# Two-layer attention with experts and a spiking FFN: two heads' outputs packed in 32 rows, another order of the attention slot, one Sigmoid pass for spikes, the last normalisation on GpSimd

## What is computed

```python
x = x + L0_xattn(layernorm(x), ctx, ctx)      # softmax attention, 16 heads of width 8, with biases
x = x + L0_ffn(layernorm(x))                  # 8 experts, top 1, silu, 128 -> 512 -> 128
x = x + L1_xattn(layernorm(x), ctx, ctx, positions, mask)
x = x + L1_ffn(layernorm(x))                  # spiking
```

```python
m = max(scores);  e = exp(scores - m);  attn = e / (1.0 + sum(e))
out = (attn @ V) @ W_o.T
```

```python
mem_new = 0.9 * mem + y - (mem > 1)           # from mem = 0
spk = (mem_new > 1)
result = sum of the five spk / 5
```

## Time and profile before

| | us |
|---|---|
| median of 3 runs | 438.39 (435.57 to 439.0) |
| the profiled execution | 439.88 |
| its span | 438.0 |
| PE busy | 344.5 (79%) |
| DVE busy | 309.1 (71%) |
| ACT busy | 268.8 (61%) |
| POOL busy | 136.8 (31%) |
| mean granted clock of PE | 0.878 |

### The profile page before, as it was taken

One profiled execution on the slowest core, in us unless ns is written; L12 is line 12 of the kernel. 1 busy time (PEld: TensorE's weight loads), 2 busy tenths in 40 slices (PEclk: granted clock), 3 DMA queues, 4 the chain that ended last, 5 costly groups with the idle time before them and its releaser, 6 DMA issues.

```text
span 438.0 us, 9507 instructions
## 1 busy us (share of the span) xinstructions
PE 344.5 (79%) x3230; PEld 205.2 (47%) x3230; DVE 309.1 (71%) x840; ACT 268.8 (61%) x473; POOL 136.8 (31%) x238
## 2 busy tenths in 40 slices
PE   1589999999897625999932679999999888796762
PEld 0233454445343514999920224545444343575751
DVE  5787999998957365466514777999998752268764
ACT  2128988889767201665511148898988785367776
POOL 4423123534002005644037455444642101011000
PEclk9999999999979855899975556999999995889996
DMA  5134342333201402554112122111221000000001
GB/s 150 55 84 127 101 121 67 108 106 88 65 4 53 138 19 43 144 146 100 42 51 67 56 60 59 49 47 49 60 68 56 5 6 1 0 1 13 15 22 48
DMA packets 35920, 27.36 MB, mean 62 GB/s; under 512 B 5936, under 2 KB 31920, under 8 KB 35872
## 3 DMA queue, kind: packets, MB, share of 16 engines
q1 hardware_dynamic: 32896, 23.51, 18.7%
q0 software_dynamic: 1248, 2.56, 2.7%
q10 hardware_dynamic: 1728, 0.66, 0.6%
HBM read 14.19 MB, written 4.13 MB: 42 GB/s over the span
## 4 chain that ended last, share of the span: by engine, by line
PE 55%; DVE 18%; ACT 11%; issue 6%; DMA 5%; POOL 4%; SPq 0%; ACTq 0%; DVEq 0%; POOLq 0%
PE M L338 14%; PE S L287 11%; DVE nm L656 9%; PE S L1234 5%; PE S L1253 4%; ACT Pt L513 3%; PE S L1410 3%; PE M L446 2%; PE M L454 2%; PE M L346 2%; DMA sorted_y<-ysb 2%; PE M L1426 2%; ACT spike L1472 2%; PE M L409 2%; PE S L1434 1%
## 5 line engine op out<-in xcount | busy, mean ns | idle before, releaser
L656 DVE TENSOR_REDUCE nm<-S 128x2 f32<-128x512 f32 x256 | 164.5, 686 | 31.3 <-PE S L287 29.1
L513 ACT ACTIVATE Pt<-S 128x1024 f32<-128x1024 f32 x128 | 130.3, 1019 | 35.8 <-PE S L296 33.7
L287 PE MATMUL S<-Kt,Qt 32*128 32x256 f16 x512 | 86.9, 303 | 18.3 <-DVE nm L656 8.4
L296 PE MATMUL S<-Qt,Kt 32*128 32x256 f16 x512 | 79.1, 290 | 0.0
L338 PE MATMUL M<-Pt,Vt 128*32 128x256 f32 x1024 | 74.5, 412 | 1.5 <-ACT Osb L500 0.9
L287 PEld LDWEIGHTS S<-Kt,Qt 32*128 32x128 f16 x512 | 25.1, 95 | 74.4 <-DVE nm L656 49.1
L338 PEld LDWEIGHTS M<-Pt,Vt 128*32 128x32 f32 x1024 | 28.0, 114 | 29.4 <-issue 6.5
L632 POOL TENSOR_TENSOR rstd<-ve,mhalf 128x2 f32<-128x2 f32 x24 | 17.8, 743 | 63.0 <-DVE ve L610 62.4
L1279 ACT ACTIVATE hf<-S,b1c 128x128 f32<-128x128 f32 x92 | 26.1, 369 | 18.4 <-PE S L1234 18.4
L815 POOL TENSOR_TENSOR q_lo<-qf,q_hi 128x256 f16<-128x256 f32 x15 | 10.1, 671 | 74.5 <-ACT q_hi L546 74.5
L1151 POOL DMA_INDIRECT xt<-normed_x,source x23 | 22.4, 974 | 34.6 <-DVE source L1069 17.0
(11 more groups left out here) (173 smaller groups left out, 574.0 us busy)
## 6 DMA issues: line engine op xcount, KB each, us to landing
w_ff<-in_w SPq DMA_DIRECT2D x8, 512.0 KB, 3.9
ctxT<-in_ctxT SPq DMA_DIRECT2D x16, 128.0 KB, 2.6
Pt<-in_mask SPq DMA_DIRECT2D x8, 256.0 KB, 3.0
Qt<-q_hi SPq DMA_DIRECT2D x28, 64.0 KB, 1.9
Kt<-k_hi SPq DMA_DIRECT2D x28, 64.0 KB, 1.9
sorted_y<-ysb SPq DMA_DIRECT2D x23, 64.0 KB, 2.7
Kt<-k_lo SPq DMA_DIRECT2D x16, 64.0 KB, 1.9
Qt<-q_const SPq DMA_DIRECT2D x16, 64.0 KB, 2.6
```

What stands on the lines that cost most here:

```text
L287: mm = pe.matmul(S1[h % 2][:, q, :], Qt[b % NBUF][rows_of(h), h // HG, q * P:(q + 1) * P], Kt[b % NBUF][rows_of(h), h // HG, :], start=Tru ...
L296: mm = pe.matmul(S2[pair % 2][:, hh, k, :], Kt[b % NBUF][rows_of(h), h // HG, k * P:(k + 1) * P], Qt[b % NBUF][rows_of(h), h // HG, :], st ...
L513: act.activation(Pt[i // 2][:, 2 * j:2 * j + 2, :].rearrange("p a n -> p (a n)"), S2[i % 2][:, :, :, :].rearrange("p a k n -> p (a k n)"), ...
L656: v.tensor_reduce(nm[par][:, h // 8, :, h % HG, h // HG % 2], S1[h % 2][:, :, :], AX.X, ALU.max, negate=True)\
```

## The change

Five things change.

1. **Packing.** Two groups of heads share a block of 32 rows, 16 for each. Vt has a new layout, so that `pv` of the second group adds into the same rows as the first. The four `pv` of a tile all go to M[1]. ACT copies the bank once, 128x512, where it copied four times 128x256. Four transposes follow where there were eight, and one reciprocal and one multiplication of double width. The rows of wo and the bias of V are put into the order of `packed_order()` on the host.
2. **PE's order.** The transposes of the outputs all stand after pair 1. `op` and `v` follow pair 4, `op` first. The next `m_turn` follows pair 5, then `pv` 0; `pv` 1 follows pair 6, `pv` 2 pair 7 and `pv` 3 the first pair of the next slot.
3. **ACT's and DVE's order.** kf and k_hi stand ahead of aT. ACT takes the copy of V, behind exp(4), and the copy of the maxima behind it. DVE adds to X behind r(4); the moments stand behind r(5).
4. **Spikes.** One Sigmoid of `SPIKE * mem - (SPIKE + 128)`, written in f16 with SPIKE = 1.75 * 2**30, takes the place of Relu and Sign; it stands first in ACT's slot, and is cut in two for the last tile. One more table is loaded on ACT.
5. **The last normalisation.** xn of the FFN is made on POOL. PE's wait for the last X moves from before the first h to before y.

```diff
             def pv(b, par, g):
                 pe.wait_ge(ly["exp_done"], 8 * b + 2 * g + 2)
-                if g == 0:
-                    pe.wait_ge(ly["v_copied"], b + 1)
+                tile, sub = g // 2, g % 2
                 for k in range(QT):
                     for i in range(HG):
-                        mm = pe.matmul(M[O_BANK[g]][32 * i:32 * i + 32, 0:S], Vt[par][:, k, HG * g + i, :],
-                                       Pt[g][:, i, k * S:(k + 1) * S], start=(k == 0), stop=(k == QT - 1))
+                        at = (k * NPK + tile) * 2 * (HG * KB + KH) + sub * HG * KB + i * KB
+                        mm = pe.matmul(M[1][KB * i:KB * i + KB, tile * S:(tile + 1) * S], Vflat[par][:, at:at + KB],
+                                       Pt[g][:, i, k * S:(k + 1) * S], start=(sub == 0 and k == 0),
+                                       stop=(sub == 1 and k == QT - 1))
...
                 pair(4)
-                if nxt and ly["bias"]:
-                    next_m_turn()
-                if cur:
-                    if old:
-                        pe.wait_ge(ly["aT_copied"], b)
-                    elif ly["bias"]:
-                        pe.wait_ge(ly["ob_made"], 1)
-                    pv(b, par, 0)
-                if nxt and ly["position"]:
-                    next_m_turn()
-                pair(5)
...
                 if old:
-                    if cur:
-                        pe.wait_ge(ly["o_copied"], 4 * b + 1)
                     pe.wait_ge(ly["aT_copied"], b)
...
+                if nxt:
+                    if new:
+                        pe.wait_ge(ly["k_copied"], b + 3)
...
                     mm.then_inc(ly["v_done"], 1)
+                pair(5)
+                if nxt:
+                    pe.wait_ge(ly["v_copied"], b + 2)
+                    m_turn(b + 1, par1, 0)
                 if cur:
                     if old:
                         pe.wait_ge(ly["x_added"], b)
...
+                    pv(b, par, 0)
+                pair(6)
+                if cur:
+                    pv(b, par, 1)
+                if ffn and s == B - 1:
+                    ffn_start(ffn, -3)
+                pair(7)
+                if cur:
                     pv(b, par, 2)
...
                 exp(3)
+                if new and not keys_ahead(ly, s):
+                    keys_on_scalar(act, ly, b, nxt)
...
+                exp(4)
+                if nxt:
+                    act.wait_ge(ly["v_done"], b + 2)
...
+                    act.activation(Vheads[1 - par][:, :, :, 0:DH],
+                                   M[0][:, 0:S].rearrange("p (a i d) -> p a i d", i=HG, d=DH), ACT.Copy) \
+                       .then_inc(ly["v_copied"], 1)
                     m_copy(b + 1, 0)
...
                 r(4)
-                if ahead and cur:
-                    norm_moments(v, b + 3, ly["norm_own"], ly["xvar"], applied(b + 3))
+                if old:
+                    v.wait_ge(ly["op_done"], b)
...
+                    v.tensor_tensor(x, M[1][:, 0:S], x, ALU.add).then_inc(ly["x_added"], 1)
...
         def ffn_on_gpsimd(pool):
             for b in range(B):
                 norm_root(pool, b, ff["var"], ff["rstd"])
+                if b >= 2:
+                    pool.wait_ge(ff["xT"], b - 1)
+                norm_apply(pool, b, xn[b % 2], ff["rstd"], ff["xn"])
...
                 if exists(s, -1):
...
+                    cuts = (0, STEPS - 1, STEPS) if s == B else (0, STEPS)
+                    for start, end in zip(cuts, cuts[1:]):
+                        act.wait_ge(ff["mem"], 2 * (STEPS - 1) * (b - 1) + 2 * (end - 1))
+                        act.activation(spike[1 - par][:, start:end, :], mem[1 - par][:, start:end, :], ACT.Sigmoid,
+                                       bias=spike_bias[:, :], scale=SPIKE).then_inc(ff["spike"], 1)
```

208 lines of the change are left out of this document (85 added, 123 removed).

## The result

The changed kernel took 442.16 us (median of 20 runs, 439.12 to 450.22), the kernel before 438.82 beside it (20 runs). The ratio is 1.0076, with a 95% interval of 1.0051 to 1.0102: 3.3 us slower, where 1.9 us faster was forecast. The time lies inside the stated range of 428 to 446, in the part that stood for "within 1%". The profiled execution has a span of 442.3 us, 4.3 more than the 438.0 of before.

What follows compares the result with a forecast made beforehand. The prediction took loops of waits, not a full engine, as the bound. Its terms, 3.6 + 4.9 - 1.0 - 5.0 - 0.5 - 2.9 - 1.0 = -1.9, took 438.4 to 436.5 us; own range 431 to 442, widened to 428 to 446.

Steps and rivals of the forecast that it cites:

- The terms for the steady slots: Attention slots of both layers: later copies and moments lengthen them, +3.6 us in layer 0 and +4.9 in layer 1.
- the term for layer 1's tail: Last slots of layer 1: one transpose round less and PE kept busy so the clock stays up, -5.0 us (-1.0 to -6.4).
- layer 0's tail: Last slots of layer 0: one round less saves its wait of 0.68 and half the transposes' 0.66, -1.0 us.
- the sum of the FFN: Spiking FFN: -0.5 for the moved wait for X, -2.9 for the body, -1.0 for the end.
- What bounds the kernel: Whole kernel: no engine is full; the wait that ends last in each stage's loop counts, such as a late ACT copy.
- The rival that took the engines' sums for the gain (A): Attention slots: each gets shorter by what DVE is relieved of, at most 0.6 us; 421 to 428 us, chance 0.19.
- The steady slots of layer 0: Seven slots: PE waits 0.93 before `op` for aT's late copy; +0.39 or +0.6 us each, +3.6 in all.
- The steady slots of layer 1: Six slots: late moments delay POOL and so m_turn, +1.37 us in each of three slots, +4.9 in all.
- rival B: Steady slots: PE's new pauses bring the clock down, 2.2 us a fall; 443.1 for three, 445.3 for four; chance 0.20.
- The body's term: FFN tiles: ACT's single pass and xn off DVE cut the 6.36 us loop; half of -5.8 taken for contention, -2.9.
- The rule of the Trainium skill: FFN body: port lock lets POOL's xn shut out DVE's membrane, +2.1 us, 441.5 in all; as a rival, chance 0.10.
- The end: FFN from the last membrane's start to the last fin: about 7.0 us where 7.98 stood, -1.0.

Runs made afterwards that it cites:

- the kernel of the last experiment: Changed kernel with aT copied ahead of kf and k_hi, moments behind r(4) in layer 1 only, FFN's xn on DVE: 424.63 us, 0.968 of before.

## Why the prediction was right or wrong, point by point

**The step that failed.** The terms for the steady slots counted PE's new pauses as time and put their effect on the clock at nothing, and the term for layer 1's tail counted 5.4 us for a clock that would stay up. The runs showed the reverse: between the first and last `op` of the two layers the half-rate time grew by 6.8 and 6.5 us, with three falls in steady slots that cost about 2.5 us together, and the tail kept its share. The second step is layer 0's tail, taken for 1.0 shorter: from `op` to `op` its last two slots last 13.55 and 13.25, for 11.81 and 10.69. That the order of copies lengthens the steady slots was right, and so was the sum of the FFN, though by errors that cancel. The time lies within the stated range, but in the part given to no change, and on the other side of the kernel before.

**What bounds the kernel.** Right. DVE lost 12 us of work and ACT 16, and the kernel became slower. The rival that took the engines' sums for the gain (A) fell.

**The steady slots of layer 0.** Right in place, and in size for a slot at full clock: the wait ahead of `op`, released by ACT's aT, is there, 0.69 to 0.72 for my 0.93, and these slots last 13.68 and 13.97 to 13.99, for 13.78 and about 14.0. That the sum came out (+4.0 for +3.6) is luck. It has six slots for my seven, and 1.9 of it are the fall and the one slot of 14.87, lengthened by DVE's shift beside POOL; neither was in my sum. The last slot, with 6.8 us at half rate in both kernels, gave 0.5 back.

**The steady slots of layer 1.** The mechanism was right to a tenth: +1.39 in a slot at full clock, where +1.37 was forecast, with m_turn's wait ended by POOL. The term came out 2.7 larger all the same. Of these, 1.5 are two slots with a fall of the clock, 0.8 the slot before the tail, and the rest small differences in the others.

**The clock in steady slots.** The prediction named the mechanism as rival B, with a chance of 0.20, and argued against it from slots with waits of 0.2 to 0.5 at 1.00, though its own schedule had PE standing still for 0.93. Rows about short waits say nothing of long ones. The price was off the other way: I took 2.2 a fall from the slot at 113.24, whose half-rate stretch lasted 6.8 us; a fall of 3.4 us within a slot cost 0.77 and 0.98, less than half its length; that waits of the slot absorb a part is my reading and not shown. Three falls, then, gave about 2.5 in the trace, and not the 6.6 of that rival.

**The start.** Forecast 0, measured +1.8. PE's rows run there at the slow duration (0.39 for a score product) and change to 0.28 at 41.42 in the kernel before and at 46.29 in the changed one; in the kernel of the last experiment at 43.23. I did not cost the first slots at all. But little of the 1.8 is a loss: the first `op` of full slots begins at 55.69 and 55.79, and what differs is how much of the slot lies ahead of pair 1. The second trace of the kernel before changes at 44.48 and has that `op` at 57.02, the two further ones of the changed kernel change at 45.17 and 45.30 and have it at 54.67 and 54.80. So one execution differs from another by 1.1 to 1.3 us here, and a loss at the start is not shown.

**The tails.** The term of layer 1 came out, -6.1 for -5.5, but not for its reason. The clock did not stay up: the changed kernel has 6.8 us at half rate in slot 6 and 6.8 in the tail, where before had 3.4 and 10.2 (10.8 in the prediction's coarser reading), so the same 13.6. What I counted as 5.4 of clock came from the clock in small part only: 3.4 us at half rate moved into the slot before, which became 0.8 longer. The lower end of the range, -1.0 with the clock as it was, had missed the work that the new order does before that pair 1: by the last `op` but two to the last, both kernels take nearly the same, 27.7 and 27.2. So most of the -6.1 is the cut, and by `op` the tail gained 0.5, for 5.0 forecast. In layer 0 the -1.0 became +1.0: a fall of 3.4 us at 141, and the 0.7 ahead of `op`, which I had costed in the steady slots only. By `op` its last two slots are 4.3 longer. In the last one all four `pv` stand behind the `op` at 140.31, where before the first of them (134.45) stood ahead of the `op` at 136.09. The tail's term did not follow this.

**The FFN.** The body's term was under-sized, -4.8 for -2.9. I took half for contention on DVE, and there was little: membrane instructions beside POOL's xn kept 0.42 to 0.48 in most cases, two in each of two tiles took 0.55 to 0.56, and it was POOL's xn that was stretched, from 1.57 to between 1.89 and 2.11. And the gain has another source than mine: Sigmoid alone, with xn still on DVE, makes the body 33.88, the change 34.62. The rule of the Trainium skill ("SBUF — State Buffer", section "SBUF: two separate sides"), by which whichever instruction comes first shuts the other out for its whole length, would have given +2.1 here, and the FFN's traces don't bear that out. A DVE instruction that ends with POOL's is seen elsewhere, in the shift of 1.37 us; whether it is the same rule no run here shows. What I costed at nothing was xn's way to PE: ahead of the first membrane the move costs 1.06, and in the body it takes back what it gives. The stretch from the last `op` to the first membrane is still 0.1 shorter than before, with the moved wait for X and a granted clock of 0.85 for 0.62 on its side; how much each gave is not shown. The table load of 1.28 was hidden, as said. The end gave 0.8 to its last fin for the forecast's 1.0, and lost 1.1 behind it: 3.76 from the start of the last fin to the end, for 2.68. All kernels with the new attention and xn on POOL have 3.5 or more there, those with xn on DVE 2.7, but the old attention with xn on POOL has 2.75 too, so its cause stays open.

**The sum.** Of the 6.2 between forecast and span, 3.1 are the steady slots, with three falls of about 2.5 in them, 1.8 the start, 2.0 layer 0's tail, which has a fall in its number too, and 2.3 the FFN's beginning and last store. The body (1.9), layer 1's tail (0.6) and the experts (0.5) go the other way. Cut by `op`, the same 6.2 is 6.4 of all ahead of the FFN (+8.9 for +2.5), less 0.2 in the FFN (-4.6 for -4.4).
